# Local attention on one NeuronCore: who adds the window mask to the scores, and who copies the first tile's transposed probabilities

## The reference, cut to what matters

```python
q = l2norm(q) * qs                       # per head, 64 wide
k = l2norm(k) * ksc
q, k = rotary_xpos(q, k)
# windows of 64 queries; each looks at its own window and the one before
sim = jnp.einsum('bhwid,bhwjd->bhwij', bq * QK_SCALE, bk)
mask = (i < j) | (i > j + WINDOW) | (j == -1)
sim = jnp.where(mask, -jnp.finfo(sim.dtype).max, sim)
attn = jax.nn.softmax(sim, axis=-1)
out = jnp.einsum('bhwij,bhwjd->bhwid', attn, bv)
x = x + out.reshape(b, n, INNER) @ wo    # then a gated MLP
```

## Time and profile before

| what | value |
|---|---|
| median of 3 runs | 3981.91 us (3971.15 to 3981.96) |
| the profiled execution's own time | 3975.32 us |
| its span, first to last instruction | 3973.5 us |
| mean granted TensorE clock | 0.988 |
| local attention, layer 0 | about 806 to 1400 us of the span |
| local attention, layer 1 | about 1568 to 2172 us of the span |
| steps in it | 35 for each layer, 32 of them with scores |

### The profile page before, as it was taken

How to read it: one execution, slowest core, us unless ns; L and a number is a source line. 1 busy time by engine, 2 the same in 40 slices (tenths; PEclk the granted TensorE clock), 3 DMA queues, 4 the chain that set the end, 5 groups by cost and what they waited for, 6 DMA issues and landing times. The chain is left out here.

```text
span 3973.5 us, 103557 instructions
## 1 busy us (share of the span) xinstructions
PE 3778.9 (95%) x34587; PEld 2912.5 (73%) x34841; DVE 2908.7 (73%) x6982; ACT 2654.1 (67%) x6409; POOL 1950.9 (49%) x1930
## 2 busy tenths in 40 slices
PE   7999999889999999999999999999999999999999
PEld 5767767657777765777776567777777777789998
DVE  6999999878888856888887855555655565656666
ACT  6999999868888833788886356666666666633333
POOL 4666666667777712667675433343334333411111
PEclk9999999989999989999999999999999999999999
DMA  3000000000000010000000100000000000000000
GB/s 107 1 0 0 0 0 0 1 22 21 20 24 20 20 28 20 14 16 13 16 13 19 31 26 1 0 0 0 0 0 0 0 0 0 0 7 9 9 9 9
DMA packets 69052, 47.64 MB, mean 12 GB/s; under 512 B 38361, under 2 KB 57953, under 8 KB 68833
## 3 DMA queue, kind: packets, MB, share of 16 engines
q1 hardware_dynamic: 68960, 46.43, 4.6%
HBM read 12.62 MB, written 4.19 MB: 4 GB/s over the span
## 5 line engine op out<-in xcount | busy, mean ns | idle before, releaser
L1871 ACT ACTIVATE l_probs<-l_act,l_neg_max 128x128 f32<-128x128 f32 (+1 forms) x1024 | 415.5, 425 | 274.0 <-DVE l_neg_max L1820 271.3
L1799 POOL TENSOR_TENSOR l_probs<-l_probs,l_sums 128x512 f32<-128x512 f32 x384 | 391.0, 1039 | 366.9 <-DVE l_sums L1828 366.9
L613 POOL TENSOR_TENSOR t_probs<-t_probs,t_neg_max 128x512 f32<-128x512 f32 x384 | 391.1, 1040 | 247.4 <-DVE t_neg_max L682 247.2
L1820 DVE TENSOR_REDUCE l_neg_max<-l_act 128x2 f32<-128x512 f32 (+1 forms) x384 | 247.0, 685 | 353.4 <-PE l_act L1983 160.7
L2197 ACT ACTIVATE e_hT<-e_act 128x512 f32<-128x512 f32 x256 | 152.7, 597 | 287.0 <-PE e_act L2218 287.0
L672 DVE SCALAR_TENSOR_TENSOR t_probs<-t_tanh_qk,scalars_sb,t_dve 128x512 f32<-128x512 f32 x384 | 269.7, 744 | 72.8 <-ACT t_tanh_qk L787 42.8
L1084 POOL TENSOR_TENSOR w_invQ<-w_lengthsQ,minus_half 128x16 f32<-128x16 f32 x64 | 243.8, 3810 | 87.8 <-DVE w_lengthsQ L1157 87.8
L2230 PEld LDWEIGHTS e_dve<-e_sb,e_hT 128*128 128x128 f32 x2048 | 269.6, 192 | 16.2 <-ACT e_hT L2197 3.0
L1071 POOL TENSOR_TENSOR w_swappedQ<-w_rawQ,w_table 128x512 f32<-128x512 f32 x128 | 162.1, 1288 | 242.9 <-ACT w_rawQ L1269 242.9
L2230 PE MATMUL e_dve<-e_sb,e_hT 128*128 128x128 f32 x2048 | 270.7, 275 | 2.6 <-ACT e_hT L2197 2.6
L2218 PE MATMUL e_act<-e_xnT,e_sb 128*128 128x256 f32 x1024 | 266.7, 383 | 0.0
(11 more groups left out here) (257 smaller groups left out, 10283.5 us busy)
## 6 DMA issues: line engine op xcount, KB each, us to landing
w_v_mid<-w_v SPq DMA_DIRECT2D x128, 130.0 KB, 2.3
z<-w_z_copy SPq DMA_DIRECT2D x32, 128.0 KB, 2.0
h<-z SPq DMA_DIRECT2D x32, 128.0 KB
out<-x_sb SPq DMA_DIRECT2D x32, 128.0 KB, 1.8
h<-z SPq DMA_DIRECT2D x32, 127.0 KB
wqkv_sb<-L_ffn_wqkv SPq DMA_DIRECT2D x2, 768.0 KB, 6.7
kv_up_sb<-L_attn_w_kv_up SPq DMA_DIRECT2D x1, 1024.0 KB, 9.5
e_sb<-L_ffn_w SPq DMA_DIRECT2D x1, 1024.0 KB, 5.5
```

Source lines behind the costliest of these rows:

```text
L613: nc.gpsimd.tensor_tensor(p, p, neg_max[:, j, 0:len(gs)].unsqueeze(2) .broadcast_to((P, len(gs), P * (t + 1))), ALU.add).then_inc(shifted. ...
L1799: nc.gpsimd.tensor_tensor(p, p, sums[:, at, 0:len(hs)].unsqueeze(2) .broadcast_to((P, len(hs), P * (t + 1))), ALU.mult).then_inc(divided.s ...
L1820: nc.vector.tensor_reduce(neg_max[:, units.index(name), 0:len(hs)], to_act.bank("s" + name, back)[:, :].rearrange("p (h j) -> p h j", h=le ...
L1871: ins = nc.scalar.activation(probs[:, at % SLOTS, s * width:(s + 1) * width], bank[:, s * width:(s + 1) * width], ACT.Exp, bias=neg_max[:, ...
```

## The change

TensorE no longer writes the mask; the first score matmul of each bank starts the accumulation. VectorE adds the mask to both score banks at once, reading and writing PSUM (128x1024, the bf16 mask broadcast over the two sides), and its maximum waits for that add through a new semaphore. VectorE's copy of tile 0's transposed probabilities goes; ScalarE makes it between its copy of Q and `exps(1)`. `scores(1)` has no wait of its own any more; the wait for y1 ahead of it covers it.

```diff
+    mask_order = ["0", "1"]
+        masked = Count(sem("masked"), mask_order, [], mask_order)
...
+                def mask_added(t, back):
+                    job = f"S{t}"
+                    of[job].wait_filled(dve, job, back)
+                    scores = of[job].bank(job, back)[:, :].rearrange("p (s e) -> p s e", s=SIDES)
+                    nc.vector.tensor_tensor(
+                        scores, scores, masks[:, t].rearrange("p i j -> p (i j)").unsqueeze(1)
+                        .broadcast_to((P, SIDES, PAIRS * P)), ALU.add).then_inc(masked.sem, 1)
+
                 def maxima(t, back):
                     job = f"S{t}"
-                    of[job].wait_filled(dve, job, back)
+                    dve.wait_ge(masked.sem, masked.done(str(t), back))
...
                     if back:
+                        mask_added(0, back)
                         maxima(0, back)
...
                     if back:
+                        mask_added(1, back)
                         maxima(1, back)
-                        ring_a.wait_filled(dve, "P0", back)
-                        nc.vector.tensor_copy(pT[:, 0].rearrange("p s i q -> p (s i q)"),
-                                              ring_a.bank("P0", back)[:, :]).then_inc(ring_a.drained.sem, 1)
...
                     if front:
                         raw_taken("Q", front)
                     if back:
+                        taken("P0", back, pT[:, 0].rearrange("p s i q -> p (s i q)"))
                         exps(1, back)
...
-                def masked(t, back):
-                    job = f"S{t}"
-                    of[job].wait_free(pe, job, back)
-                    for side in range(SIDES):
-                        nc.tensor.matmul(of[job].bank(job, back)[:, side * BANK:(side + 1) * BANK],
-                                         c["ident_bf"][:, :], masks[:, t].rearrange("p i j -> p (i j)"),
-                                         start=True, stop=False)
-
                 def scores(t, back):
                     job = f"S{t}"
+                    if t == 0:
+                        of[job].wait_free(pe, job, back)
...
-                                    kT[dims, i, keys], start=False, stop=i == PAIRS - 1)
+                                    kT[dims, i, keys], start=i == 0, stop=i == PAIRS - 1)
...
                     if back:
-                        masked(0, back)
                         ring_b.wait_drained(pe, "QT", back)
                         scores(0, back)
...
                     if back:
-                        masked(1, back)
                         scores(1, back)
```

## The result

The changed kernel takes 4041.5 us (median of 4 runs, 4039.5 to 4045.5), the kernel before 3980.9 in the same comparison: ratio 1.0169, 95% interval 1.0153 to 1.0186. It is 1.7% **slower**. The profiled execution took 4042.52 us, its span is 4040.7: 67.2 us more than before.

What follows compares the result with a forecast made beforehand. The loop PE, ACT, PE, DVE, ACT, PE was taken to bound each step; the add, less the bias or PE's lead, plus the copy's wait gave 31 x 2.30 = 71 us, forecast 4048 us, range 4016 to 4085.

Steps and rivals of the forecast that it cites:

- the sum: Steady steps: +0.99 us in layer 0 and +1.31 in layer 1, times 31 steps, 71 us on 3975.3.
- The chain: One step's loop PE, ACT, PE, DVE, ACT, PE is as long as the step, 18.50 us in layer 0.
- The add's price: Tile 0's mask add on VectorE, between score bank and maximum: 1.36 us on the chain, bounds 1.15 and 1.66.
- The first bias: Layer 0's small bias multiply, moved behind GpSimd's sine products, takes 0.17 instead of 0.73: 0.56 us back.
- The two mask matmuls of tile 1: Taken off TensorE ahead of scores(1), they bring its earliest output projection forward by 0.52 us, which becomes idle time.
- The copy on ScalarE: Copy of tile 0's probabilities behind the Q copy makes attended(0) wait: 0.19 us a step, bounds 0 and 0.3.
- The handoff: From ScalarE's copy end to PE's start 0.19 us, so attended(0) can start 2.13 us after hT ends.
- its saved 0.5 us becomes idle time: TensorE, ready at about 14.3, would wait some 1.3 us for hT in front of the output projection.
- TensorE as the bound: Rival: PE bounds at its output projection, steps shrink by up to 0.52, 32 us, to 3950; chance 0.04.
- The add held by GpSimd: Rival: GpSimd's sine products of K hold VectorE's add, 61 us in layer 0, about 4149 total; chance 0.05.
- The clock: Rival: PE's waits lower its clock for output projection, values and K projection, 4.8 us a step, near 4340; chance 0.05.

Runs made afterwards that it cites:

- e5: Changed kernel with tile 0's mask added twice on VectorE in each step; 4127.8 us, ratio 1.0389 to the kernel before.
- e3: Changed kernel with tile 0's mask back on TensorE, tile 1's add and ScalarE's copy kept; 3978.7 us, ratio 1.0009 to the kernel before.
- e4: Changed kernel with tile 1's mask back on TensorE, tile 0's add and ScalarE's copy kept; 4038.4 us, ratio 1.0159 to the kernel before.
- e9: As e8, but with both tiles' masks on TensorE and nothing added on VectorE; ratio 0.9988 to the kernel before.
- e8: Changed kernel, tile 0's mask on TensorE, ScalarE order hT, copy of Q, probabilities copy, squares of Q; VectorE's residual add ahead of lengths of Q; 3944.7 us.
- e1: Changed kernel with all masks back on TensorE and no adds; only the copy of tile 0's probabilities stays on ScalarE; 3983.7 us, ratio 1.0021.
- e11: As e1, but ScalarE copies tile 0's probabilities right behind hT, ahead of the copy of Q; ratio 0.9981 to the kernel before.
- e2: Changed kernel with the copy of tile 0's probabilities back on VectorE behind bias 1, both adds kept; 4062.4 us, ratio 1.0215.
- e7: Changed kernel, tile 0's mask on TensorE, ScalarE's copies of hT and tile 0's probabilities ahead of the squares of Q; 3970.8 us, ratio 0.9994.

## Why the prediction was right

Forecast 4048 us, range 4016 to 4085; measured 4041.5. Against the profiled execution the sum said +71 us and it was +67.2. Point by point:

**The chain.** Right. Predicted offsets in layer 0 were 10.25 for the exponentials, 15.62 for hT, 19.49 for the step; they are 10.09, 15.47 and 19.37. In layer 1: 10.30, 15.67, 19.54 against 10.21, 15.59 and 19.50. e5 shows the add on the chain with its full length, e3 and e4 show that it is tile 0's add and that one alone.

**The add's price, taken as 1.36.** Mis-sized by 0.09: add to maximum is 1.27 (1045.75 to 1047.02), the row itself 1.23. Writing PSUM and the bf16 operand added nothing to the 1.22 of the SBUF rows. Over 62 steps that is 5.6 us, more than the 4 us by which the sum was too high; smaller misses of both signs, below, made up the difference, so the sum's closeness is partly luck. The nearest row's distance had two waits in it, not one; which of them made up the 0.09 no run shows. On the Trainium skill's statement (VectorE: DVE Perf Modes, "The DRAIN you can't avoid") that a semaphore between two DVE instructions costs nothing extra: after the scaling of K (1.23 long) the next add, whose bank has long been full, starts 1.14 later (1051.08 to 1052.22); between add and maximum, which waits for it, it is 1.26 to 1.27. So a wait on VectorE's own last result cost some 0.12 here; the trace doesn't agree with the skill's statement, and the measurement decides.

**The first bias, 0.56 back in layer 0.** Right: 0.17 after, against 0.73 in the earlier trace rows. It is why layer 0 lost less (0.89) than layer 1 (1.27). In layer 1 nothing came back at the bias; the 0.24 us by which hT could have been earlier there took off that much instead, and the copy's place added as much again.

**The two mask matmuls of tile 1, worth 0.52 of lead.** They cost 0.43: from y1's transposes to `scores(1)` it is 0.53 after, 0.96 before. e9 less e8 says 0.43 again. In the changed kernel it is all idle time, as predicted. Tile 0's were put at nothing, for TensorE waits for the transposed Q either way. Nearly so: `scores(0)` starts at 6.21 into the step with them (before, e1, e3) and at 6.16 without (after, e4), and in layer 0, where VectorE waits for the scores, its first instruction on them starts at 7.36 instead of 7.42. In layer 1 that gains nothing, VectorE is busy until 7.50 either way.

**The copy on ScalarE, 0.19 a step.** The handoff was right: `attended(0)` starts 2.10 after hT's end (2.13 predicted). The last values then take 1.80 instead of 1.74, a term that the sum didn't have and whose cause no run shows, so the move costs 0.23 to 0.25 (e1), for its place behind the copy of Q (e11: nothing). Summed for layer 0: -0.09 (add), -0.06 (earlier scores), -0.03 (handoff), +0.06 (values) make the 0.12 by which the predicted step, 19.49, was too long.

**What failed beside the forecast.** "its saved 0.5 us becomes idle time, some 1.3 us in front of that projection": TensorE's wait splits, 0.55 in front of the z transposes and 0.69 in front of the output projection in layer 0, 0.67 and 0.69 in layer 1. I overlooked that z's transposes take the bank that V1 leaves, and ScalarE copies V1 out only behind the late exponentials. It moved no time, as ScalarE reached hT later still, but what the prediction said the profile would show ("from 0.22 to about 1.3 us") is wrong. The maximum starts 1.27 behind the add, just under the 1.3 to 1.4 foretold, and "no other stage changes" holds only to the 4 us above. The idle share of PE is 9 of 100 us instead of the 12 I had worked out.

**The rivals.** TensorE as the bound: out, its share fell. It is right for another kernel, e8, where the chain is shorter. The add held by GpSimd: out; the first add of layer 0 takes 1.23 (1045.75) in the midst of the sine products (1044.40, 3.36 long). By the Trainium skill's rule (GPSIMD Engine Reference, the table row on SBUF interfaces) an instruction with one SBUF operand isn't held, and the trace agrees with it; the same rule covers K's product in e2 and the clip in e7, both with two, and both were held. The clock: in the steady steps the granted clock stays 1.00 with PE idle 9 us in 100 and single waits of 0.7, so what the Trainium skill (Perfetto Trace Analysis, "Matmul Optimizations") warns of did not come at this size.

## What to carry to other kernels

Before work is moved off the engine that is busiest, close the loop of one step in the timeline and ask on which side of it the new home lies: TensorE was 97% busy, and still an instruction of 1.27 us between a score bank and its maximum cost 1.27 us a step, while the same one 6 us later was free. Split such a move by place: the mask that lay in a shadow should have stayed, the other paid its full 0.43 us a step once ScalarE's order no longer held TensorE back (e8, 0.74% below the kernel before). And where whole-kernel times differ by less than half a per cent, compare the repeated step, and look at the opening steps too: in e11 they alone were 4.4 us shorter.

## What the hardware showed that I had not expected

When VectorE's product with two SBUF operands and GpSimd's product meet, a tenth of a microsecond goes with a long or a short row: with GpSimd 0.10 ahead the DVE row is 2.25 long instead of 1.22, with both at 1925.55 it is 1.22. In layer 1 of e2 the loop settled into two step lengths in turn, 20.40 and 19.28, to the end of the layer.

A DVE `tensor_tensor` that reads and writes a 128x1024 fp32 score bank in PSUM takes 1.22 to 1.23 us, no more than one from SBUF to SBUF. In layer 0 GpSimd's sine products ran beside it.
